# Down products of a routed block moved as a whole behind the next block's up products

## What is computed

```python
# ffn0: the one expert of 8 with the highest score
h = silu(xn @ W1[e] + b1[e]); ye = h @ W2[e] + b2[e]        # 256 -> 1024 -> 256
out = ye * top1_score
# ffn2: two experts of 8, hidden width 704, and a shared expert
y = sum(comb[:, e] * (silu(xt @ w1[e]) * (xt @ w3[e])) @ w2[e])
out = y + (silu(x @ sw1) * (x @ sw3)) @ sw2
# ffn3: two experts of 7, hidden width 704, and a shared expert, the same form
```

## Time and profile before

| what | us |
| --- | --- |
| median of 3 runs | 789.73 (788.59 to 790.14) |
| the profiled execution | 787.2 |
| its span, first to last instruction | 785.4 |
| TensorE busy | 683.5 |
| VectorE busy | 351.6 |
| ScalarE busy | 255.3 |
| routed part of ffn0, from the first up product to the last down product | 90.2 to 177.6 |
| routed part of ffn2 | 464.2 to 576.0 |
| routed part of ffn3 | 660.1 to 763.8 |

### The profile page before, as it was taken

The page is one execution under the profiler, slowest core; times in us unless marked ns, Lnnn a source line. Parts: engine busy times, 40 slices in busy tenths (PEclk is TensorE's granted clock), DMA queues, the critical chain, the costliest instruction groups (busy, mean ns, idle before and its releaser), DMA issues.

```text
span 785.4 us, 15607 instructions
## 1 busy us (share of the span) xinstructions
PE 683.5 (87%) x6255; PEld 520.7 (66%) x6303; DVE 351.6 (45%) x1035; ACT 255.3 (33%) x639; POOL 133.1 (17%) x100
## 2 busy tenths in 40 slices
PE   8998769998866798989988979999957995999996
PEld 6665558885433346765754669888945564988885
DVE  3328630005999785667668521111137742111113
ACT  1342235453633404653682312222210111222221
POOL 2000200001299700131050220000040040000004
PEclk9999879999999999999999989999987998999999
DMA  8960279925455130000003788999150555899913
GB/s 305 387 227 0 76 245 338 366 86 205 139 151 151 44 121 0 1 1 0 1 0 111 309 296 310 349 369 359 59 180 1 211 224 161 326 350 372 353 50 90
DMA packets 30931, 143.81 MB, mean 183 GB/s; under 512 B 4625, under 2 KB 16721, under 8 KB 24337
## 3 DMA queue, kind: packets, MB, share of 16 engines
q1 hardware_dynamic: 23888, 132.86, 46.4%
q0 software_dynamic: 2240, 5.90, 2.3%
q10 hardware_dynamic: 4736, 4.13, 1.6%
HBM read 133.15 MB, written 9.71 MB: 182 GB/s over the span
## 4 chain that ended last, share of the span: by engine, by line
PE 51%; DVE 19%; issue 11%; DMA 8%; POOL 7%; ACT 4%; SPq 1%; DVEq 0%; POOLq 0%; ACTq 0%
PE PS L549 48%; DVE arena L2033 5%; POOL x_slots L1502 3%; DMA x_slots<-XH,posu 2%; DMA TMP<-x_slots 2%; DMA arena<-y_slots,posu 2%; PE PS L608 2%; POOL arena L1515 2%; PE PS L572 1%; DVE stats L1596 1%; DVE stats L1589 1%; POOL arena L1541 1%; DVE arena L2158 1%; DMA y_slots<-arena 1%; DMA arena<-bc_scratch 1%
## 5 line engine op out<-in xcount | busy, mean ns | idle before, releaser
L549 PE MATMUL PS<-arena 128*64 128x64 f32 (+5 forms) x3188 | 241.5, 265 | 10.9 <-DVE arena L2161 3.1
L549 PEld LDWEIGHTS PS<-arena 128*64 128x64 f32 (+1 forms) x3188 | 202.2, 155 | 42.5 <-issue 15.4
L1819 DVE TENSOR_TENSOR arena<-arena,PS 128x384 f32<-128x384 f32 (+1 forms) x66 | 26.9, 407 | 186.6 <-ACT arena L1197 186.6
L549 PE MATMUL PS<-warm 128*128 128x512 bf16 (+2 forms) x377 | 92.6, 362 | 20.0 <-DVE rs L1580 15.3
L1515 POOL DMA_INDIRECT arena<-y_slots,posu x25 | 23.6, 944 | 321.7 <-DMA y_slots<-arena 315.0
L549 PEld LDWEIGHTS PS<-warm 128*128 128x128 bf16 (+1 forms) x425 | 38.7, 101 | 58.1 <-DVE rs L1580 18.5
L1197 ACT ACTIVATE arena<-PS 128x384 f32<-128x384 f32 (+1 forms) x66 | 27.2, 413 | 138.7 <-PE PS L549 138.7
L1528 POOL TENSOR_TENSOR arena<-arena 128x1152 f32<-128x1152 f32 x16 | 56.4, 3522 | 33.5 <-DVE arena L2033 33.5
L549 PE MATMUL PS<-arena,wsh 128*128 128x128 f32 (+3 forms) x568 | 58.0, 272 | 1.3 <-ACT arena L1189 0.7
L549 PE MATMUL PS<-arena,ident 128*128 128x512 f32 (+1 forms) x128 | 38.0, 440 | 21.5 <-POOL arena L1528 21.5
L549 PEld LDWEIGHTS PS<-arena,wsh 128*128 128x128 f32 (+1 forms) x568 | 51.7, 178 | 5.9 <-issue 2.8
(11 more groups left out here) (306 smaller groups left out, 913.7 us busy)
## 6 DMA issues: line engine op xcount, KB each, us to landing
arena<-w_moe SPq DMA_DIRECT2D x24, 2176.0 KB, 9.4
arena<-w_moe SPq DMA_DIRECT2D x9, 2052.0 KB, 9.7
wsh<-w_moe SPq DMA_DIRECT2D x8, 2176.0 KB, 10.6
arena<-bc_scratch SPq DMA_DIRECT2D x32, 288.0 KB, 3.8
wsh<-w_moe SPq DMA_DIRECT2D x3, 2052.0 KB, 11.2
y_slots<-arena ACTq DMA_DIRECT2D x19, 128.0 KB, 9.3
wx<-w_moe SPq DMA_DIRECT2D x1, 2176.0 KB, 18.4
wx<-w_sh SPq DMA_DIRECT2D x1, 2176.0 KB, 8.9
```

Source lines behind the costliest of these rows:

```text
L549: return nc.tensor.matmul(out_, l, r, start=start, stop=stop, skip_group_check=True)
L1819: ins = v.tensor_tensor(firsts(hid_b[x][:, 0:full], n_), firsts(sg_s[x][:, 0:full], n_), firsts(PS[:, 2 * x + 1, 0:full], n_), ALU.mult)
```

## The change

- TensorE's order for block b becomes: up half 0, the turn of block b+1, up half 1, both down halves of block b-1. The last block's two down halves follow behind the loop.
- `up` waits, for b > 0, until the activation of the same half of block b-1 is written, which used to be implied by the order.
- There is a second pair of `hid_b` buffers, chosen by p, laid over the shared expert's activation buffers. VectorE clears the unused part of both.
- Rows of a large block are turned by eight product instructions on two column tiles of 64 (`x_on_tiles`) where the block at hand is small; else as before.
- ScalarE's order becomes silu 0, x_copy of b+1, silu 1, y_copy of b-1, y_store of b-1.

```diff
-        hid_b = [take(512) for _ in range(2)]
+        hid_b = [[take(512) for _ in range(2)]]
...
+        hid_b += [[part(o - 4 * SHW, 512), part(o - 2 * SHW, 512)]]
...
+                def x_on_tiles(b, p):
+
+                    pe.wait_ge(sem("x1"), 16 * USE_X[name]["P"])
+                    for d in range(KD):
+                        for c in range(2):
+                            last = mm(PS[64 * c:64 * (c + 1), 7 - p, SB * d:SB * (d + 1)],
+                                      rows_of(name, b)[:, 128 * d + 64 * c:128 * d + 64 * (c + 1)], ident[:, :])
+                    last.then_inc(sem("xt_t"), 1)
...
                     if x == 0:
                         pe.wait_ge(sem("xbT"), b + (at + 1))
+                    if b:
+                        pe.wait_ge(sem("hid2"), 2 * b + (2 * at + x - 1))
...
                 def emit(b, hb, p, kind, before, after):
                     up(b, p, 0, kind)
-                    if before:
-                        down(b - 1, 1 - p, 1, before)
-                    elif name != "ffn0":
+                    if not before and name != "ffn0":
                         pe.wait_ge(sem("side_added"), STAGE[name] + 1)
                     if not before and name in ONE_HOT:
                         x_chosen(1)
+                    elif after == "P" and kind == "S":
+                        x_on_tiles(b + 1, 1 - p)
                     elif after:
                         x_transposes(b + 1, 1 - p, after)
                     up(b, p, 1, kind)
-                    down(b, p, 0, kind)
+                    if before:
+                        for x in range(2):
+                            down(b - 1, 1 - p, x, before)
...
-                down(nb - 1, (nb - 1) % 2, 1, "P")
+                for x in range(2):
+                    down(nb - 1, (nb - 1) % 2, x, KINDS[name][nb - 1])
...
                     silu(b, p, 0, kind)
+                    if after:
+                        x_copy(b + 1, 1 - p, after)
+                    silu(b, p, 1, kind)
                     if before:
                         y_copy(b - 1, hb - 1 + p, 1 - p, before)
-                    if after:
-                        x_copy(b + 1, 1 - p, after)
-                    if before:
                         y_store(b - 1, 1 - p, before)
-                    silu(b, p, 1, kind)
...
-                link(v.memset(hid_b[1][64:128, part_chunk:3 * SB], 0.0))
+                for p in range(2):
+                    link(v.memset(hid_b[p][1][64:128, part_chunk:3 * SB], 0.0))
```

More of the change, by code:

```diff
@@ L661, in down @@
                         if kind == "P":
-                            last = mm(PS[:, 4 + p, 0:D], hid_b[x][:, SB * c:SB * (c + 1)], wd[:, D * c:D * (c + 1)], start, stop)
+                            last = mm(PS[:, 4 + p, 0:D], hid_b[p][x][:, SB * c:SB * (c + 1)], wd[:, D * c:D * (c + 1)], start, stop)
                         else:
                             for h in range(2):
-                                last = mm(PS[64 * h:64 * (h + 1), 4 + p, 128 * h:128 * (h + 1)], hid_b[x][:, SB * c:SB * c + HB],
+                                last = mm(PS[64 * h:64 * (h + 1), 4 + p, 128 * h:128 * (h + 1)], hid_b[p][x][:, SB * c:SB * c + HB],
                                           wd[:, D * c + 128 * h:D * c + 128 * (h + 1)], start, stop)
@@ L1201, in silu @@
                         for c in range(HC[name][x]):
-                            last = nc.scalar.activation(hid_b[x][:, SB * c:SB * c + n_], PS[:, 2 * x, SB * c:SB * c + n_],
+                            last = nc.scalar.activation(hid_b[p][x][:, SB * c:SB * c + n_], PS[:, 2 * x, SB * c:SB * c + n_],
                                                         ACT.Silu, bias=weights_of(name, b)[:, o_ + c:o_ + c + 1])
@@ L1248, in routed @@
                 over_blocks(name, emit, between if name in ONE_HOT else None)
-                y_copy(nb - 1, (nb - 1) // 2, (nb - 1) % 2, "P")
-                y_store(nb - 1, (nb - 1) % 2, "P")
+                y_copy(nb - 1, (nb - 1) // 2, (nb - 1) % 2, KINDS[name][nb - 1])
+                y_store(nb - 1, (nb - 1) % 2, KINDS[name][nb - 1])
             def shared(name, steps, halves=(0, 1)):
@@ L1818, in emit @@
                         full = HU[name][x] // 128 * SB
-                        ins = v.tensor_tensor(firsts(hid_b[x][:, 0:full], n_), firsts(sg_s[x][:, 0:full], n_),
+                        ins = v.tensor_tensor(firsts(hid_b[p][x][:, 0:full], n_), firsts(sg_s[x][:, 0:full], n_),
                                               firsts(PS[:, 2 * x + 1, 0:full], n_), ALU.mult)
                         if full < 3 * SB:
-                            ins = v.tensor_tensor(hid_b[x][0:64, full:full + n_], sg_s[x][0:64, full:full + n_],
+                            ins = v.tensor_tensor(hid_b[p][x][0:64, full:full + n_], sg_s[x][0:64, full:full + n_],
                                                   PS[64:128, 2 * x, full:full + n_], ALU.mult)
```

## The result

The changed kernel takes 792.78 us (median of 8 runs, 790.95 to 793.26), the kernel before 789.95 beside it (8 runs). The ratio is 1.0031, with a 95% interval of 1.0018 to 1.0044: 2.5 us slower, in an interval of 1.4 to 3.5 (the medians themselves are 2.83 apart). The forecast was 790.6, in a range of 787.2 to 793.6: the time lies inside, 2.2 us above the forecast, and on the side that had the chance 0.38. The loss is about three times the 0.85 us that was forecast.

The account below looks back on a forecast made before the run. TensorE, busy 87% of the span, was taken as the bound, weight DMA close behind. ffn0 +3.6, ffn2 -0.9 and ffn3 -1.85 gave +0.85 us on the median 789.73: 790.6, range 787.2 to 793.6.

Parts of the forecast that it names:

- the side that had the chance 0.38: Whole kernel: slower by over 0.2%, above 791.3 us, chance 0.38; within 0.2% had 0.45, faster 0.17.
- The pair: TensorE, one small plus one large block: 12.62 us instead of 12.90, a net gain of 0.28.
- changes of shape: Within a pair: five changes between 128*64 and 128*128 products cost 0.17 us each; the new order keeps two, gaining 0.50.
- ffn3 gives back 1.85 us in full: ffn3: 1.85 us gained, six pairs giving 1.65, since everything behind hangs on the same last down product.
- ffn2: ffn2: store 0.66 us later, but shared-weight load issued 1.85 sooner, so gathers land sooner and VectorE's adds end 0.9 earlier.
- ffn0: ffn0: +3.6 us; block 3 starts 0.7 later, block 11 starts 1.2 late waiting for weights, its store comes 10.41 after that.
- The second rival: All three stages: weight loads over 12.6 us set the pace; ffn0 +5.2, ffn2 0, ffn3 -0.5, about 794.4; chance 0.13.
- the wait of 1.29 us ahead of block 11: ffn0, kernel before: TensorE's 1.29 us idle before block 11's up was read as already a wait for weights.
- The sum for ffn0: ffn0: +3.6 us up to block 11's store, paid in full as that store opens the gathers and VectorE chain.
- What costs nothing: New activation wait before up halves (at most 1.5 us per block if uncovered), ScalarE's later copies, larger VectorE clear (under 0.1).

Follow-up runs that it names:

- e5: Changed kernel, but large blocks' rows turned by two plain transposes again instead of eight products on column tiles: 792.72 us, ratio 1.0064 to the kernel before.
- e10: e8 plus products on zeros ahead of the first routed rows in all three stages: 783.29 us, ratio 0.9939 to the kernel before.
- e12: e11 with ffn0's new order, except block 0's and block 11's down halves right behind the next block's first up half: 782.52 us, ratio 0.9926 to kernel before.
- e9: e8 plus the load of the shared weights in ffn2 waiting until the gathers have landed: 784.59 us, ratio 0.9945 to the kernel before.
- e1: Changed kernel with ffn0 put back to the old order, new order in ffn2 and ffn3 alone: 786.56 us, ratio 0.9986 to the kernel before.
- e7: Changed kernel plus twelve more products on zeros right behind ffn0, order untouched: 791.84 us, ratio 1.0043 to the kernel before.
- e2: Changed kernel with ffn2 and ffn3 put back to the old order, new order in ffn0 alone: 793.92 us, ratio 1.0074 to the kernel before.
- e8: e1 plus block 15's down products in ffn2 ahead of block 16's second up half, so stored earlier: 786.84 us, ratio 0.9972 to the kernel before.
- e11: e9 plus products on zeros ahead of the first routed rows in all three stages: 782.03 us, ratio 0.9919 to the kernel before.

## Why the prediction was right, and where it was off

**The pair.** 12.62 forecast, 12.62 measured, and the turn on column tiles 0.44 for 0.44. The sum from neighbours of the same kind held to the last digit, and e5 shows that its reason, changes of shape, is the right one (0.15 each, forecast 0.17).

**ffn3.** -1.85 forecast, -1.52 measured. The step "ffn3 gives back 1.85 in full" held but for the clock at its head: the half clock lasted 4.5 us behind the rows in the changed kernel (664.3 to 671.1, rows at 666.58) and 3.5 before, 0.5 us of work. With the clock held up (e10 to e12) the same stage takes 101.90.

**ffn2.** -0.9 forecast, -0.32 measured. The mechanism was right, which e9 shows by taking the load away. The store came 0.53 us later (0.66 forecast) and the load of the shared weights was issued 2.0 sooner (1.85), but VectorE's adds ended only 0.3 sooner and not 1. The size was not sure by half a microsecond: the load took 9.6 us, where the sum had 8.9 (574.3 to 583.2), which is more than the 0.58 us that are missing. In e1 it took 8.8, and the stage gained 1.2.

**ffn0.** +3.6 forecast, +3.58 measured, and by the steps given: block 3 started 10.79 us behind the rows (10.72 forecast), block 11's load was issued 46.9 behind them (46.5) and took 10.4 (11.0), the block started 57.3 behind them (57.5), and its store came 10.57 later (10.41). The other kernels of this order show the agreement as partly luck: they took 68.66, 70.34 and 70.92, so +4.4 to +6.6. In e7 the load for block 11 took 12.4 us, in e2 that of block 6 took 12.0. The second rival, the ring run dry, is true of ffn0 in these two. Of ffn2 and ffn3 it is false: no wait there is put down to weights, in any of the kernels. The time met the upper end of the range with 0.8 us to spare.

One reading was wrong, without moving the sum: that the wait of 1.29 us ahead of block 11 is already one for weights. Its row names ScalarE's copy of the block's rows, which ended at 164.8, and the weights (153.2, 11.1 to landing) were there at 164.3. In the old order that copy stands behind the copy of block 9's output, which waits for a store. e1, which has the old order there, shows it whole, on ScalarE and then on TensorE:

```profile
164.75 0.56 ACT L1249 ACTIVATE arena<-PS 64x128 f32<-64x128 f32 x2 [3.18 <-DMA y_slots<-arena]
165.55 0.31 ACT L1224 ACTIVATE arena<-PS,colv 128x64 f32<-128x64 f32 x1
165.96 2.03 PE L559 MATMUL PS<-arena 128*64 128x64 f32 x48 [1.99 <-issue]
```

Block 11's weights were there at 164.5 (issued 153.59, 10.9 to landing), 1.4 us before TensorE went on, and so it is in e8 to e11. The change took this wait away together with TensorE's order. ScalarE's new order with TensorE's old one in ffn0, which might give up to 1.4 us by this estimate, was not run.

**The term that was missing.** The sum for ffn0 ended with the store, and everything behind it was carried along at its old length. It grew by 1.1 us here and by 1.9 in e2 to e5, since a store that moves back against TensorE's own last products makes TensorE idle, and that idle time costs clock. The four terms make +2.85 with it, +1.74 without it, and +0.85 was forecast; the other 0.9 is ffn2's and ffn3's shortfall. The profile before held the warning: the products on zeros stood there, and an idle time of 1.63 us behind them.

**What costs nothing.** In the changed kernel the new wait ahead of each up half never shows as a releaser, nor do ScalarE's copies behind the second activation. (In e10 and e11 one wait of 0.58 and 0.95 us, early in ffn2, is put down to VectorE's activation product; what ended it isn't shown.)

## What to carry over

A reordering within an engine is worth the changes of shape and the turns that it saves, and that can be read off neighbours to a few hundredths. What it costs is to be sought where other queues hang on single points of the old order: the point at which a ring's buffer comes free, the last store, and the idle time of TensorE behind each, which has to be priced with the clock that it loses. The best kernel here takes the new order in the two stages whose ring has room, leaves the third alone, keeps a bulk load out of the way of the gathers that end a stage, and fills TensorE's known waits with products on zeros. It still has the wait of ScalarE's copy ahead of block 11 of ffn0.

## What the hardware showed

- TensorE's clock: behind ffn0 it stayed full after idle times of 0.94 to 1.76 us, and was at half after 3.45 to 3.49; inside ffn0 it was at half after 2.95 (e7). About 2 us went both ways: it stayed full after 1.99 in e1 and after 2.01 and 2.02 in e10, and fell in e12 after 2.03 inside ffn0 and, about 1 us into the work behind it, after 2.00 behind ffn0. In attn2 it fell in two kernels of fourteen behind idle times of 1.05 us and less. Behind ffn0 it stayed at half for 3.2 us in the changed kernel and for 5.9 in e2. Filling 6 us of idle time with products whose result nobody reads kept it full in the heads of three stages.
- A change between products of 128*64 and 128*128 costs TensorE 0.15 us, and turning 128x256 float32 by eight products on column tiles 0.44 us, twice the two plain transposes. The Trainium skill (page "TensorEngine Tiling (Array Packing)", section "Key Properties") says that a change of the tiling mode drains the engine; the trace agrees and gives the price.
- The time to the last landing of a 2.1 MB load in ffn0 ran from 8.4 us (e10, e11) to 12.6 (e2); the mean DMA share of a pair there was 0.93 before and 0.92 after the change.
- A gather of rows took 2.7 us alone (e9) and up to 8.4 us when it was issued just behind a load of 2.2 MB (changed kernel).
